# Edge logits through a DRAM table instead of one-hot matmuls in a graph network kernel

## The chip, the cores and the metric

The kernel runs on one core of a Trainium2 chip. The metric is device time in microseconds (us) for one execution. The engines of the core are PE (TensorE, matrix products; PEld is its weight load), DVE (VectorE), ACT (ScalarE), POOL (GpSimd) and SP (SyncE, here only a queue of transfers). DMA transfers run beside them.

## The reference, cut to what matters

512 nodes with 1024 features and 8192 edges, sorted by destination. The edges are of three kinds by their position: the first 256 are `hh`, the next 1280 `oo`, the last 6656 `ho`. Only the attention part concerns the change:

```python
h = relu(layernorm(x))
feat  = concat([h[src], h[dst]])                 # per edge, 2048 wide
e     = relu(feat @ W_kind + b_kind)             # one weight per kind of edge
logit = (e @ W_a + b_a)[:, 0]
m     = segment_max(logit, dst);  ex = exp(logit - m[dst])
alpha = ex / segment_sum(ex, dst)[dst]
z     = segment_sum(alpha[:, None] * h[src], dst)
out1  = x + relu(concat([h, z]) @ W_node + b_node)   # W_hn for the first 128 rows, W_on for the others
# then a second graph layer on out1: layernorm, relu, one linear map, sums with degree weights
```

Two edges of one kind with the same source and destination have the same logit. So the kernel keeps, for each kind, a dense 512 x 512 matrix of logits (destination by source) and one of edge counts, and does the softmax and the sum over edges as dense matrix work.

## The kernel before, in words

**Tables.** `feat @ W_kind` is split into a source half and a destination half. For each of the three kinds and each half, PE multiplies all 512 nodes, so an edge needs only one row of `tab_a` (source) and one of `tab_b` (destination, bias added), both in DRAM. That is 12 *edge chunks* of PE work (numbers 0 to 11: kind, half, half of the columns), then four *node chunks* (12 to 15) for the upper halves of `W_on` and `W_hn`. A chunk has 8 *steps* (k = 0 to 7); a step is one 256 KB weight load on SP's queue into one of 8 slots of `raw` (L247), a rounding to a high part on ACT (L448), the low part on DVE (`low_w`, L897), and 12 matmuls on PE (L646; fewer in a node chunk). ACT or DVE copies each finished bank to `stage` (L466, L905) and ACT's queue stores it, 1 MB per edge chunk. A load is released by the low part 8 steps before it, so the loads follow DVE's order.

**Counts.** In chunks 2 to 5 DVE makes two 0/1 matrices per tile of 128 edges (`count_onehots`), and PE sums their products into the counts.

**Gathers.** There are 64 tiles of 128 edges: 52 `ho`, 10 `oo`, 2 `hh`, in that order. For tile q POOL issues an indirect DMA that fetches 128 rows of `tab_a` (4 KB each) into one of 8 slots of `gath` (`gather_src`, L308) and, when that has landed, a second one that fetches 128 rows of `tab_b` and adds them in SBUF (`gather_dst`, L315), three tiles later in the order. Before each `gather_src` POOL copies the tile's indices to `tabl_s` (L305). DVE's `edge(q)` (L912) then does relu, the product with `W_a` and the row sum, which gives 128 logits in `lg[:, q]`, and frees the slot.

**Sums.** The logits go to the dense matrix by matmul. DVE splits them into three bf16 parts (`split_logits`, L918 to L923) and makes two one-hot matrices (`logit_onehots`, L929); ACT scales one by each part (`logit_parts`, L495); PE adds three products per tile, 12 per step being the weights' own (`add_logits`, L596). DVE also prepares the inverse of the counts (L935, L936) and a mask for pairs without an edge (L941), which PE adds (`open_masked`, L615), and at the end of each kind multiplies and takes row maxima (`copy_kind`, L947). Tables of numbers (`SUM_AT`, `EDGE_AT`, `ONEHOT_AT`, `SPLIT_AT`) say at which chunk and step each of these stands: seven tiles per chunk in chunks 6 to 11, the rest in chunks 12 to 15, and `edge(q)` 12 steps ahead of its sum.

**After that.** DVE combines the row maxima (L1021 to L1023; `nmx` is the last), ACT takes exponentials, DVE the row sums, and from there the kernel is one chain: attention product, node update, second layer, output. Nothing of it is touched by the change.

Of the kernel before, what the change touches and what calls it, by code (L numbers as in the profile page):

```python
# [5 lines left out]
P = 128  # L25
# [19 lines left out]
def gnn_kernel(nc, x, src, dst, W_hh, b_hh, W_oo, b_oo, W_ho, b_ho, W_a, b_a,  # L45
# [12 lines left out]
    with ExitStack() as ctx:  # L58
# [8 lines left out]
        def sb(name, shape, dt, size=None, over=None, shift=0):  # L67
# [6 lines left out]
            else:  # L74
# [16 lines left out]
        G, TC = 8, 7  # L91
        topsum = sb("topsum", [P, NM, D], F32)
        onehot = sb("onehot", [P, OS, 4, N], BF16, over="topsum")
# [13 lines left out]
        GROUPS = {g: -(-ET // g) for g in (G, TC)}  # L107
        pow8 = sb("pow8", [1, G, G + 3], F32)
        code_row = sb("code_row", [1, ET + G], F32)
        code_w = sb("code_w", [1, ET + G], F32)  # L110
        pack_f = sb("pack_f", [1, G + 3], F32)

        pack_i = {g: sb(f"pack{g}_i", [1, GROUPS[g]], I32) for g in (G, TC)}
        node_f = sb("node_f", [P, ET, 3], F32)
        tabl_f = sb("tabl_f", [P, ET, 2], F32, over="logit_d", shift=20 * P)
        tabl_i = sb("tabl_i", [P, ET, 2], U32)
        tabl_s = sb("tabl_s", [P, GB, 2], U32)
        lg = sb("lg", [P, ET], F32)
        lgr = sb("lgr", [P, ET], F32)
        lgp = sb("lgp", [P, 3, ET], BF16)  # L120
        lgs = sb("lgs", [P, 3, ET], F32)
# [26 lines left out]
        mask_b = [sb("mask_ho", [P, NM, N], BF16, over="logit_d", shift=4 * (2 * NM * N + 2 * N)),  # L148
                  sb("mask_oo", [P, NM, N], BF16, over="bias2", shift=4 * D),
                  sb("mask_hh", [P, NM, N], BF16, over="bias2")]  # L150
# [7 lines left out]
        top_d = nc.dram_tensor("top_d", [N, D], F32).ap()  # L158

# [13 lines left out]
        s_mask = sem("masks_ready")  # L173
        s_part = sem("onehot_parts_ready")
# [18 lines left out]
        s_stg = sem("index_staged")  # L193
        s_seen = sem("index_seen")
        s_oh = sem("onehots_ready")
        s_ohu = sem("onehot_slots_free")
        s_kind = sem("kind_counted")
        s_kfree = sem("kind_banks_free")
# [27 lines left out]
        TILES = (T_HO, T_OO, T_HH)  # L226
        CH_EDGE = 3 * 2 * NN
# [45 lines left out]
        def _(pool):  # L273
# [10 lines left out]
                           allow_small_or_imprecise_dtypes=True).then_inc(s_gconst, 1)  # L284
            for j in range(G):
                nc.gpsimd.memset(pow8[:, j, :], float(8 ** j)).then_inc(s_gconst, 1)
            nc.gpsimd.memset(code_row[:, :], 0.0).then_inc(s_gconst, 1)
            nc.gpsimd.memset(ones[:, :], 1.0).then_inc(s_gconst, 1)
            for m in range(NM):
                pool.wait_ge(s_x[m], 16)  # L290
            pool.dma_start(wa_b[:, :], W_a.rearrange("d a -> a d").partition_broadcast(P)).then_inc(s_const, 16)
# [10 lines left out]
            def gather_src(q, s, kinds):  # L302

                pool.wait_ge(s_edge, q + 1)
                nc.gpsimd.tensor_copy(tabl_s[:, s, :], tabl_i[:, bass.ds(q, 1), :].rearrange("p a b -> p (a b)")).then_inc(s_stg, 1)  # L305
                pool.wait_ge(s_stg, q + 1)
                pool.sem_inc(s_seen, 1)
                pool.indirect_dma_start(out=gath[:, s, :], out_offset=None, in_=tab_a[0:kinds * N, :],  # L308
                                        in_offset=bass.IndirectOffsetOnAxis(ap=tabl_s[:, s, 0:1], axis=0)).then_inc(s_ga[s], 16)

            def gather_dst(s, u, kinds):

                pool.wait_ge(s_ga[s], u * 16 + 16)
                pool.sem_inc(s_seen, 1)
                pool.indirect_dma_start(out=gath[:, s, :], out_offset=None, in_=tab_b[0:kinds * N, :],  # L315
                                        in_offset=bass.IndirectOffsetOnAxis(ap=tabl_s[:, s, 1:2], axis=0),
                                        compute_op=ALU.add).then_inc(s_g[s], 16)
# [5 lines left out]
            def gather_run(first, end, kinds, pending=0):  # L323

                for q in range(first, end):
                    gather_src(q, q % GB, kinds)
                    if q - LAG >= first - pending:
                        gather_dst((q - LAG) % GB, (q - LAG) // GB, kinds)

            def gather_rest(end, kinds):  # L330
                for q in range(end - LAG, end):
                    gather_dst(q % GB, q // GB, kinds)

            LAG = 3
            for i in range(4):
                pool.wait_ge(s_st[i], 32)
            for q in range(GB):
                gather_src(q, q, 1)
            tables_landed(1)
            pool.wait_ge(s_copied, NM + NM * 4)  # L340
            for q in range(GB - LAG):
                gather_dst(q, 0, 1)
            bias(0, b_hh)
            with pool.Fori(1, T_HO // GB) as i:
                for s in range(GB):
                    gather_src(i * GB + s, s, 1)
                    gather_dst((s - LAG) % GB, i if s >= LAG else i - 1, 1)
            gather_run(T_HO // GB * GB, T_HO, 1, LAG)
            gather_rest(T_HO, 1)
            tables_landed(2)  # L350
            gather_run(T_HO, T_HO + T_OO, 2)
            gather_rest(T_HO + T_OO, 2)
            tables_landed(3)
# [5 lines left out]
            pool.wait_ge(s_ohu, OS + 2 * ET)  # L359
# [29 lines left out]
        SUM_AT = {(6 + i, k): i * TC + k for i in range(6) for k in range(TC)}  # L389
        SUM_AT |= {(12, k): 42 + k for k in range(8)}  # L390
        SUM_AT |= {(13, k): 50 + k for k in range(2)}
        SUM_AT |= {(13, 4 + k): 52 + k for k in range(4)}
        SUM_AT |= {(14, k): 56 + k for k in range(6)}
        SUM_AT |= {(15, k): 62 + k for k in range(2)}
        assert sorted(SUM_AT.values()) == list(range(ET))

        EARLIER = 12
        EDGE_AT = {divmod(c * KT + k - EARLIER, KT): q for (c, k), q in SUM_AT.items() if q < ET - 2} | {(14, 0): ET - 2, (14, 1): ET - 1}
        ONEHOT_AT = {divmod(c * KT + k - 1, KT): q for (c, k), q in SUM_AT.items() if q < ET - 2} | {(14, 6): ET - 2, (14, 7): ET - 1}

        SPLIT_AT = {}
        for c in range(6, 16):
            tiles = [q for (c2, _), q in SUM_AT.items() if c2 == c]
            SPLIT_AT[(c - 1, KT - 1) if c < 15 else (14, 4)] = (min(tiles), max(tiles) + 1)

        SLOT, SLOT_FREE, user = {}, {}, {s: ET - OS + s for s in range(OS)}
        for (_, k), q in sorted(SUM_AT.items()):
            SLOT[q] = k % OS
            SLOT_FREE[q] = OS + user[k % OS] + 1
            user[k % OS] = ET + q  # L410
        LAST_OF_KIND = (T_HO - 1, T_HO + T_OO - 1, ET - 1)
# [7 lines left out]
        def _(act):  # L419
# [40 lines left out]
            def copy_a(q):  # L460

                for m in range(NM):
                    bank_done(act, q, m)
                    if q:
                        act.wait_ge(s_st[m], q * 16)
                    nc.scalar.copy(stage[:, m, :], ps[:, NM + m, :]).then_inc(s_copied, 1)  # L466
                    act.wait_ge(s_copied, NM + q * NM + m + 1)
                    act.dma_start(table(q, m), stage[:, m, :]).then_inc(s_st[m], 16)
# [21 lines left out]
            def logit_parts(q):  # L490

                act.wait_ge(s_oh, ET + q + 1)
                s = SLOT[q]
                for i in (1, 2, 0):
                    ins = nc.scalar.mul(onehot[:, s, 1 + i, :], onehot[:, s, 1, :], lgs[:, i, q:q + 1])  # L495
                ins.then_inc(s_part, 1)

# [7 lines left out]
            def edge_chunk(q):  # L505

                for k in range(KT):
                    if q * KT + k + AHEAD < (CH_EDGE + 4) * KT:
                        rounds(q * KT + k + AHEAD, q * KT + k + AHEAD + 1)
                    if (q, k) in SUM_AT:  # L510
                        logit_parts(SUM_AT[q, k])
# [65 lines left out]
        def _(pe):  # L577
            pe.sem_inc(s_slot, KT)
            pe.sem_inc(s_ohu, OS)
            pe.wait_ge(s_gconst, 7 + G)  # L580

            def codes(g, size):

                return nc.values_load_multi_w_load_instructions(
                    pack_i[size][0:1, bass.ds(g, 1)], engines=[mybir.EngineType.PE], min_val=0, max_val=8 ** size - 1,
                    skip_runtime_bounds_check_because="the codes are packed on the chip, 3 bits each")[1][0]

            def accumulate(code, t, s, parts):
# [5 lines left out]
                def block(j):  # L594
                    for i in range(parts):
                        mm = nc.tensor.matmul(ps[:, bass.ds((lo + j) & 3, 1), :].rearrange("p a n -> p (a n)"),  # L596
                                              onehot[:, s, 1 + i, j * P:(j + 1) * P], onehot[:, s, 0, :],
                                              start=False, stop=False, skip_group_check=True)
                    return mm
# [10 lines left out]

            def open_masked(t):

                pe.wait_ge(s_mask, t + 1)
                for b in range(NM):
# [565 lines left out]
```

## Time and profile before

| | us |
|---|---|
| median of 3 runs | 665.55 |
| the 3 runs | 665.55, 665.29, 667.62 |
| span of the profiled execution | 665.7 |

| engine | busy us | share of the span | instructions |
|---|---|---|---|
| PE | 571.4 | 86% | 2440 |
| DVE | 442.1 | 66% | 903 |
| ACT | 287.4 | 43% | 466 |
| POOL | 217.7 | 33% | 228 |

The profile gives no time of the profiled execution other than its span from the first to the last instruction; it agrees with the median of the runs. Busy times are sums over stages with different limits, so each stage has to be read by itself. A DMA share is the busy share of the 16 DMA engines; it can read a little over 1 because packets of different queues overlap.

### The profile page before, as it was taken

How to read it: one execution, taken by the hardware profiler on the slowest of the kernel's cores; microseconds unless marked ns; L12 is line 12 of the kernel's file. 1: busy time of each engine (PE TensorE's matmuls, PEld its weight loads, DVE VectorE, ACT ScalarE, POOL GpSimd, SP SyncE). 2: the span in 40 equal slices, each digit the busy share in tenths (PEclk: the TensorE clock that was granted, in tenths of full speed). 3: DMA queues.
4: the chain of work that ended last, by engine and by line, in shares of the span. 5: the costliest groups of instructions: out<-in, count | busy, mean ns of one | idle time of the engine just before them, and what ended most of it. 6: DMA issues, size and time to landing. Idle time of an engine off the chain costs nothing.

```text
span 665.7 us, 8504 instructions
## 1 busy us (share of the span) xinstructions
PE 571.4 (86%) x2440; PEld 424.7 (64%) x2441; DVE 442.1 (66%) x903; ACT 287.4 (43%) x466; POOL 217.7 (33%) x228
## 2 busy tenths in 40 slices
PE   0899999999949995969697998667949999879987
PEld 0788777776626674647475666434738788768876
DVE  6715266775776987867878975686795289872152
ACT  2623312113175554547473555589853182142110
POOL 2000230186775766667653676310030000000000
PEclk9899999999969997988989899788978899989989
DMA  8335483499999999999999999983455076030021
GB/s 316 129 111 175 135 307 122 150 224 323 301 298 314 291 314 299 310 305 317 298 318 281 323 295 308 257 226 111 128 198 213 16 247 228 2 126 0 1 79 48
DMA packets 54727, 140.53 MB, mean 211 GB/s; under 512 B 6050, under 2 KB 6178, under 8 KB 54690
## 3 DMA queue, kind: packets, MB, share of 16 engines
q0 software_dynamic: 20624, 74.98, 41.7%
q1 hardware_dynamic: 25824, 50.34, 21.8%
q10 hardware_dynamic: 8242, 14.75, 5.9%
q8 instruction: 19, 0.31, 0.2%
q14 instruction: 18, 0.15, 0.1%
HBM read 123.27 MB, written 16.78 MB: 210 GB/s over the span
## 4 chain that ended last, share of the span: by engine, by line
PE 42%; DMA 23%; POOL 12%; issue 10%; DVE 8%; ACT 3%; POOLq 1%; DVEq 0%
PE ps L646 23%; DMA gath<-tab_a,tabl_s 19%; POOL gath L315 7%; PE ps L632 6%; POOL gath L308 3%; PE ps L826 3%; DMA gath<-tab_b,tabl_s 3%; PE ps L596 3%; PE ps L782 2%; POOL tabl_s L305 2%; ACT onehot L495 2%; PE ps L803 2%; DVE logit_d L947 1%; DVE logit_d L1036 1%; PE ps L625 1%
## 5 line engine op out<-in xcount | busy, mean ns | idle before, releaser
L646 PE MATMUL ps<-ring_h,actT_h 128*128 128x512 f32 x520 | 228.3, 439 | 34.4 <-ACT stage L466 15.8
L646 PE MATMUL ps<-ring_h,actT_l 128*128 128x512 f32 x520 | 209.0, 402 | 0.0
L646 PE MATMUL ps<-ring_l,actT_h 128*128 128x512 f32 x520 | 208.4, 401 | 0.0
L495 ACT ACTIVATE onehot<-onehot,lgs 128x512 bf16<-128x512 bf16 x192 | 124.6, 711 | 104.2 <-DVE onehot L929 104.2
L646 PEld LDWEIGHTS ps<-ring_h,actT_h 128*128 128x128 f32 x520 | 101.6, 195 | 68.1 <-ACT stage L466 17.7
L315 POOL DMA_INDIRECT gath<-tab_b,tabl_s x64 | 105.7, 1652 | 95.8 <-DMA gath<-tab_a,tabl_s 40.4
L448 ACT CAST ring_h<-raw 128x512 fp32r<-128x512 f32 x160 | 94.8, 614 | 87.8 <-PE ps L646 70.7
L912 DVE SCALAR_TENSOR_TENSOR gath<-gath,wa_b 128x1024 f32<-128x1024 f32 x64 | 78.0, 1219 | 67.6 <-DMA gath<-tab_b,tabl_s 67.6
L897 DVE TENSOR_TENSOR ring_l<-raw,ring_h 128x512 fp32r<-128x512 f32 x160 | 106.6, 685 | 16.5 <-ACT ring_h L448 16.4
L646 PEld LDWEIGHTS ps<-ring_h,actT_l 128*128 128x128 f32 x520 | 101.0, 194 | 22.9
L646 PEld LDWEIGHTS ps<-ring_l,actT_h 128*128 128x128 f32 x520 | 101.8, 196 | 20.9
L596 PE MATMUL ps<-onehot 128*128 128x512 bf16 x292 | 83.8, 396 | 18.1 <-ACT onehot L495 15.7
L308 POOL DMA_INDIRECT gath<-tab_a,tabl_s x64 | 78.9, 1232 | 50.7 <-POOL tabl_s L305 47.3
L305 POOL COPY tabl_s<-tabl_i 128x2 uint32 (+1 forms) x64 | 50.1, 783 | 70.1 <-DMA tab_a<-stage 64.5
L596 PEld LDWEIGHTS ps<-onehot 128*128 128x128 bf16 x292 | 21.8, 100 | 61.3 <-issue 49.7
L848 DVE TENSOR_SCALAR onehot<-iota_f,node_f 128x512 bf16<-128x512 f16 x64 | 23.6, 369 | 31.3 <-PE ps L596 31.3
L936 DVE RECIPROCAL logit_d<-logit_d 128x512 f32<-128x512 f32 x12 | 40.2, 3353 | 0.4
L929 DVE TENSOR_SCALAR onehot<-iota_f,node_f 128x512 bf16<-128x512 f16 x128 | 39.3, 350 | 1.6 <-PE ps L596 1.2
L890 DVE TENSOR_TENSOR actT_l<-ps,actT_h 128x512 fp32r<-128x512 f32 x24 | 16.4, 691 | 31.7 <-ACT actT_h L440 31.7
L440 ACT CAST actT_h<-ps 128x512 fp32r<-128x512 f32 x24 | 14.0, 588 | 42.6 <-PE ps L632 34.7
L466 ACT COPY stage<-ps 128x512 f32<-128x512 f32 x24 | 14.0, 585 | 25.8 <-PE ps L646 19.1
L560 ACT CAST ring_h<-ps 128x512 fp32r<-128x512 f32 x16 | 8.8, 591 | 34.4 <-PE ps L782 12.7
(160 smaller groups left out, 517.3 us busy)
## 6 DMA issues: line engine op xcount, KB each, us to landing
raw<-in_L_gnn_W_ho_dram SPq DMA_DIRECT2D x32, 256.0 KB, 3.9
raw<-in_L_gnn_W_oo_dram SPq DMA_DIRECT2D x32, 256.0 KB, 6.8
raw<-in_L_gnn_W_hh_dram SPq DMA_DIRECT2D x32, 256.0 KB, 7.3
raw<-in_L_gnn_W_on_dram SPq DMA_DIRECT2D x32, 256.0 KB, 4.8
raw<-in_L_gnn_W_hn_dram SPq DMA_DIRECT2D x32, 256.0 KB, 4.0
tab_a<-stage ACTq DMA_DIRECT2D x24, 256.0 KB, 7.4
tab_b<-stage ACTq DMA_DIRECT2D x24, 256.0 KB, 8.1
w1row<-in_L_gnn_W_dram SPq DMA_DIRECT2D x2, 2048.0 KB, 8.9
```

The costliest lines, as they stand in the source:

```text
L305: nc.gpsimd.tensor_copy(tabl_s[:, s, :], tabl_i[:, bass.ds(q, 1), :].rearrange("p a b -> p (a b)")).then_inc(s_stg, 1)
L308: pool.indirect_dma_start(out=gath[:, s, :], out_offset=None, in_=tab_a[0:kinds * N, :], in_offset=bass.IndirectOffsetOnAxis(ap=tabl_s[:, ...
L315: pool.indirect_dma_start(out=gath[:, s, :], out_offset=None, in_=tab_b[0:kinds * N, :], in_offset=bass.IndirectOffsetOnAxis(ap=tabl_s[:, ...
L448: nc.scalar.copy(ring_h[:, k, :], raw[:, k % RAW, :]).then_inc(s_high, 1)
L495: ins = nc.scalar.mul(onehot[:, s, 1 + i, :], onehot[:, s, 1, :], lgs[:, i, q:q + 1])
L596: mm = nc.tensor.matmul(ps[:, bass.ds((lo + j) & 3, 1), :].rearrange("p a n -> p (a n)"), onehot[:, s, 1 + i, j * P:(j + 1) * P], onehot[: ...
L632: mm = nc.tensor.matmul(ps[:, b, :], w, v, start=(i == 0), stop=(i == len(pairs) - 1))
L646: mm = nc.tensor.matmul(ps[:, first + m, :], w, v, start=(k == 0 and i == 0), stop=(k == KT - 1 and i == 2))
L897: nc.vector.tensor_tensor(ring_l[:, k, :], raw[:, k % RAW, :], f32(ring_h[:, k, :]), ALU.subtract).then_inc(s_low, 1)
L912: nc.vector.scalar_tensor_tensor(out=gath[:, s, :], in0=gath[:, s, :], scalar=0.0, in1=wa_b[:, :], op0=ALU.max, op1=ALU.mult, accum_out=lg ...
L929: ins = nc.vector.tensor_scalar(onehot[:, SLOT[q], j, :], iota_f[:, :], node_f[:, q, e:e + 1], None, ALU.is_equal)
L936: nc.vector.reciprocal(logit_d[:, t, k, :], logit_d[:, t, k, :])
```

## The change

The sums by matmul are gone, and with them everything that prepared them: the three bf16 parts, the one-hots per logit tile, ACT's scaling, the inverse counts, the masks, the copies per kind, and the tables that placed them. The counts are still made as before.

Instead there is a table `pair_d` in DRAM with one float for each kind, destination and source (3 x 512 x 512, 3 MB). POOL fills `stage` with -1e30 at the start and stores it three times over the table. A third column of the index table holds kind x 512 x 512 + dst x 512 + src. When `edge(q)` has run, POOL scatters `lg[:, q]`, 128 floats of 4 bytes, into the table by an indirect DMA. A scatter waits until the scatter before it has landed. When all tiles of a kind are scattered, POOL reads that kind's 1 MB back into `logit_d`, and DVE takes row maxima over it with three reductions; `b_a` is added once in the maxima.

POOL's loop is written out and no longer copies indices: in each round it issues the scatter of tile q - 8, the source gather of tile q and the destination gather of tile q - 3. `edge(q)` stands at step 38 + 3q/2 of DVE's list (step 8c + k is chunk c, step k), the last four after the last chunk. ACT's first copy to `stage` waits for the fill.

```diff
-            for q in range(T_HO + T_OO, ET):
-                gather_src(q, q % GB, 3)
-            for q in range(T_HO + T_OO, ET):
-                gather_dst(q % GB, q // GB, 3)
...
+            def scatter(q):
+
+                pool.wait_ge(s_edge, GB + q + 1)
+                t = kind_of(q)
+                if q > FIRST_OF[t]:
+                    pool.wait_ge(s_sc[t], 16 * (q - FIRST_OF[t]))
+                elif t:
+                    pool.wait_ge(s_sc[t - 1], 16 * TILES[t - 1])
+                pool.indirect_dma_start(out=pair_d, out_offset=bass.IndirectOffsetOnAxis(ap=tabl_i[:, q, 2:3], axis=0),
+                                        in_=lg[:, q:q + 1], in_offset=None).then_inc(s_sc[t], 16)
+
+            def logits_back(t):
+
+                pool.wait_ge(s_sc[t], 16 * TILES[t])
+                pool.dma_start(logit_d[:, t, :, :], pairs[t].rearrange("(m p) s -> p m s", p=P)).then_inc(s_lg[t], 16)
...
+            pool.wait_ge(s_fill, 48)
+            for q in range(GB, ET + LAG):
+                if q == T_HO:
+                    tables_landed(2)
+                if q == T_HO + T_OO:
+                    tables_landed(3)
+                if q - BACK >= 0:
+                    scatter(q - BACK)
+                if q < ET:
+                    gather_src(q, 1 + kind_of(q))
+                gather_dst(q - LAG, 1 + kind_of(q - LAG))
+                if q == T_HO + T_OO - 1:
+                    logits_back(0)
+            for q in range(ET + LAG - BACK, ET):
+                scatter(q)
+            logits_back(1)
+            logits_back(2)
...
-        SUM_AT = {(6 + i, k): i * TC + k for i in range(6) for k in range(TC)}
...
+        EDGE_STEPS = [38 + q * 3 // 2 for q in range(ET)]
...
             with pe.Fori(0, 6) as i:
-                edge_chunk(i + 6, before=lambda k: uniform_sums(i, k))
+                edge_chunk(i + 6)
...
-                    if (q, k) in INVERSE_AT:
-                        inverse_counts(*INVERSE_AT[q, k])
-                    if (q, k) in MASK_AT:
-                        make_mask(MASK_AT[q, k])
-                    if (q, k) in ((13, 2), (15, 2)):
-                        copy_kind(q - 13)
-                    if (q, k) in EDGE_AT:
-                        edge(EDGE_AT[q, k])
-                    if (q, k) in SPLIT_AT:
-                        split_logits(*SPLIT_AT[q, k])
-                    if (q, k) in ONEHOT_AT:
-                        logit_onehots(ONEHOT_AT[q, k])
-                    if (q, k) == (14, 7):
-                        copy_kind(1)
-
-
-            dve.wait_ge(s_kfree, 3 * NM)
+                    for e in EDGES_AT.get((q, k), ()):
+                        edge(e)
+            for e in range(ET):
+                if EDGE_STEPS[e] >= (CH_EDGE + 4) * KT:
+                    edge(e)
+
+
+            for t in range(3):
+                dve.wait_ge(s_lg[t], 16)
+                ins = nc.vector.tensor_reduce(mx3[:, t, :], logit_d[:, t, :, :], AX.X, ALU.max)
+            step(ins)
             step(nc.vector.tensor_tensor(mx[:, :], mx3[:, 0, :], mx3[:, 1, :], ALU.max))
```

POOL's order in the middle of the gathers, before; each round is an index copy, a source gather and a destination gather:

```order
L305 COPY tabl_s<-tabl_i 128x2
L308 DMA gath<-tab_a,tabl_s 128x1024
L315 DMA gath<-tab_b,tabl_s 128x1024
L305 COPY tabl_s<-tabl_i 128x2
L308 DMA gath<-tab_a,tabl_s 128x1024
L315 DMA gath<-tab_b,tabl_s 128x1024
```

The same place after the change (its line numbers are those of the changed kernel); `pair_d<-lg` is the scatter:

```order
L305 DMA pair_d<-lg,tabl_i 786432x1
L287 DMA gath<-tab_a,tabl_i 128x1024
L293 DMA gath<-tab_b,tabl_i 128x1024
L305 DMA pair_d<-lg,tabl_i 786432x1
L287 DMA gath<-tab_a,tabl_i 128x1024
L293 DMA gath<-tab_b,tabl_i 128x1024
```

In every round the scatter stands where the copy stood, ahead of both gathers, and it waits for the landing of the scatter one round earlier.

The end of POOL's gathers after the change; the last row with x5 is scatters 59 to 63, and the x2 are the reads of the second and third kind:

```order
L305 DMA pair_d<-lg,tabl_i 786432x1
L287 DMA gath<-tab_a,tabl_i 128x1024
L293 DMA gath<-tab_b,tabl_i 128x1024
L305 DMA pair_d<-lg,tabl_i 786432x1
L293 DMA gath<-tab_b,tabl_i 128x1024
L305 DMA pair_d<-lg,tabl_i 786432x1
L293 DMA gath<-tab_b,tabl_i 128x1024
L305 DMA pair_d<-lg,tabl_i 786432x1
L293 DMA gath<-tab_b,tabl_i 128x1024
L305 DMA pair_d<-lg,tabl_i 786432x1 x5
L311 DMA logit_d<-pair_d 128x4x512 x2
```

The last destination gather is followed by five scatters in a row and two reads, where before the gathers ended POOL's part.

DVE's order ahead of `nmx` after the change (`gath,lg<-gath,wa_b` is `edge`, `ring_l<-raw,ring_h` is the low part of a weight step):

```order
L819 TENSOR_TENSOR ring_l<-raw,ring_h 128x512
L834 SCALAR_TENSOR_TENSOR gath,lg<-gath,wa_b 128x1024
L819 TENSOR_TENSOR ring_l<-raw,ring_h 128x512 x2
L834 SCALAR_TENSOR_TENSOR gath,lg<-gath,wa_b 128x1024
L819 TENSOR_TENSOR ring_l<-raw,ring_h 128x512
L834 SCALAR_TENSOR_TENSOR gath,lg<-gath,wa_b 128x1024 x5
L897 TENSOR_REDUCE mx_86<-logit_d 128x4 x3
L899 TENSOR_TENSOR mx<-mx_86 128x4
L900 TENSOR_TENSOR mx<-mx,mx_86 128x4
L901 TENSOR_SCALAR mx<-mx,ba 128x4
L902 TENSOR_SCALAR nmx<-mx,ba 128x4
```

The last low part of chunk 15 stands behind edge 58, and edges 59 to 63 and the three reductions follow it; before, edges 62 and 63 stood in chunk 14.

## Rows read from the trace of the kernel before

**Rows 1.** The page's 40 slices of the span: busy tenths, and GB/s moved.
```profile
PE   0899999999949995969697998667949999879987
DMA  8335483499999999999999999983455076030021
GB/s 316 129 111 175 135 307 122 150 224 323 301 298 314 291 314 299 310 305 317 298 318 281 323 295 308 257 226 111 128 198 213 16 247 228 2 126 0 1 79 48
```

**Rows 2.** Busy time by stage: stage, length, each engine, granted PE clock, DMA share, GB/s.
```profile
core 0: us, PE busy (x) PEld busy (x) DVE busy (x) ACT busy (x) POOL busy (x), PEclk, DMA share, GB/s
0.00:26.00 26.00, 6.44 (x32) 6.25 (x33) 16.20 (x33) 11.42 (x17) 4.78 (x24) 1.00 0.60 224
...
137.00:426.00 289.00, 247.62 (x1021) 173.38 (x1020) 218.89 (x432) 144.38 (x233) 184.84 (x171) 0.92 1.05 301
426.00:477.00 51.00, 40.42 (x152) 23.61 (x151) 36.93 (x100) 45.11 (x74) 5.05 (x3) 0.90 0.60 177
477.00:666.00 189.00, 166.01 (x758) 136.38 (x756) 113.33 (x190) 57.82 (x95) 5.91 (x11) 0.93 0.29 105
```

**Rows 3.** Vector engine in time order: first edge, last edge, `nmx` (start, duration).
```profile
136.92 1.23 DVE L912 SCALAR_TENSOR_TENSOR gath<-gath,wa_b 128x1024 f32<-128x1024 f32 x1 [0.17 <-DMA gath<-tab_b,tabl_s]
...
446.94 1.22 DVE L912 SCALAR_TENSOR_TENSOR gath<-gath,wa_b 128x1024 f32<-128x1024 f32 x1
...
476.52 0.17 DVE L1023 TENSOR_SCALAR nmx<-mx 128x4 f32<-128x4 f32 x1
```

**Rows 4.** DMA queues from 137 to 426 us (packets, MB, engine share), then two issues.
```profile
q0 software_dynamic: 16683, 60.75, 80.1%
q1 hardware_dynamic: 9659, 17.59, 17.2%
q10 hardware_dynamic: 4608, 8.39, 7.7%
...
raw<-in_L_gnn_W_hh_dram SPq DMA_DIRECT2D x32, 256.0 KB, 7.3
...
gath<-tab_b,tabl_s POOLq DMA_INDIRECT x59, 15.7
```

**Rows 5.** DMA queues from 426 to 477 us.
```profile
q1 hardware_dynamic: 3013, 5.50, 32.9%
q0 software_dynamic: 587, 2.13, 19.3%
q10 hardware_dynamic: 720, 1.31, 7.0%
```

**Rows 6.** Groups by line, whole span: count, busy us, mean ns, idle before, releaser.
```profile
L495 ACT ACTIVATE onehot<-onehot,lgs 128x512 bf16<-128x512 bf16 x192 | 124.6, 711 | 104.2 <-DVE onehot L929 104.2
...
L912 DVE SCALAR_TENSOR_TENSOR gath<-gath,wa_b 128x1024 f32<-128x1024 f32 x64 | 78.0, 1219 | 67.6 <-DMA gath<-tab_b,tabl_s 67.6
...
L596 PE MATMUL ps<-onehot 128*128 128x512 bf16 x292 | 83.8, 396 | 18.1 <-ACT onehot L495 15.7 <-issue 2.4
...
L936 DVE RECIPROCAL logit_d<-logit_d 128x512 f32<-128x512 f32 x12 | 40.2, 3353 | 0.4
L929 DVE TENSOR_SCALAR onehot<-iota_f,node_f 128x512 bf16<-128x512 f16 x128 | 39.3, 350 | 1.6 <-PE ps L596 1.2
...
L1052 DVE TENSOR_TENSOR adj<-adj,count_d 128x2048 f32<-128x2048 f32 x1 | 2.3, 2293 | 0.0
```

**Rows 7.** One round of POOL in time order (start, duration, idle before).
```profile
159.16 0.97 POOL L308 DMA_INDIRECT gath<-tab_a,tabl_s  x1 [0.79 <-POOL tabl_s L305]
160.44 1.55 POOL L315 DMA_INDIRECT gath<-tab_b,tabl_s  x1 [0.31 <-issue]
```

**Rows 8.** The page's DMA issues: count, KB each, median us from issue to landing.
```profile
gath<-in_x_dram SPq DMA_DIRECT2D x4, 512.0 KB, 5.2
top_d<-stage ACTq DMA_DIRECT2D x8, 256.0 KB, 2.6
```

More of the change, by code:

```diff
@@ L172, in gnn_kernel @@
         s_topl = [sem(f"top_loaded{m}") for m in range(NM)]
-        s_mask = sem("masks_ready")
-        s_part = sem("onehot_parts_ready")
+        s_neg = sem("empty_pairs_made")
+        s_fill = sem("pairs_filled")
+        s_sc = [sem(f"logits_scattered{t}") for t in range(3)]
+        s_lg = [sem(f"logits_loaded{t}") for t in range(3)]
         s_pool = sem("pool_chain")
@@ L321, in tables_landed @@
                     pool.wait_ge(s_st[i], 64 * kinds)
[L323 to L332, printed above, removed]
             LAG = 3
+            BACK = GB
             for i in range(4):
@@ L337, in _ @@
             for q in range(GB):
-                gather_src(q, q, 1)
+                gather_src(q, 1)
             tables_landed(1)
@@ L386, in gnn_kernel @@
         LAST_COUNTS = FIRST_COUNTS + ET // (2 * KT) - 1
-        SUM_AT = {(6 + i, k): i * TC + k for i in range(6) for k in range(TC)}
[L390 to L411, printed above, removed]
+        EDGE_STEPS = [38 + q * 3 // 2 for q in range(ET)]
+        EDGES_AT = {}
+        for q, at_step in enumerate(EDGE_STEPS):
+            EDGES_AT.setdefault(divmod(at_step, KT), []).append(q)
         def is_a(q):
@@ L579, in _, with codes, accumulate @@
             pe.sem_inc(s_ohu, OS)
-            pe.wait_ge(s_gconst, 7 + G)
-            def codes(g, size):
+            pe.wait_ge(s_gconst, 6 + G)
+            def codes(g):
                 return nc.values_load_multi_w_load_instructions(
-                    pack_i[size][0:1, bass.ds(g, 1)], engines=[mybir.EngineType.PE], min_val=0, max_val=8 ** size - 1,
+                    pack_i[0:1, bass.ds(g, 1)], engines=[mybir.EngineType.PE], min_val=0, max_val=8 ** G - 1,
                     skip_runtime_bounds_check_because="the codes are packed on the chip, 3 bits each")[1][0]
-            def accumulate(code, t, s, parts):
+            def accumulate(code, t, s):
                 lo = code >> (3 * t)
                 def block(j):
[L595 to L599, printed above, removed]
+                    return nc.tensor.matmul(ps[:, bass.ds((lo + j) & 3, 1), :].rearrange("p a n -> p (a n)"),
+                                            onehot[:, s, 1, j * P:(j + 1) * P], onehot[:, s, 0, :],
+                                            start=False, stop=False, skip_group_check=True)
                 with pe.If((lo & 4) > 0):
@@ L609, in open_banks @@
                     nc.tensor.matmul(ps[:, b, :], zeros_r[:, 0:P], zeros_r[:, :], start=True, stop=False, skip_group_check=True)
-            def open_masked(t):
-                pe.wait_ge(s_mask, t + 1)
-                for b in range(NM):
-                    nc.tensor.matmul(ps[:, b, :], ident_b[:, :], mask_b[t][:, b, :], start=True, stop=False, skip_group_check=True)
             def close_banks(done):
@@ L735, in _ @@
                     free = lambda m: pe.wait_ge(s_copied, waits[c] + (m if c == 0 else 0))
-                chunk(q + c, NM, ms, free, before=lambda k: last_sums(q + c, k))
-            pe.wait_ge(s_kfree, 3 * NM)
+                chunk(q + c, NM, ms, free)
+            pe.wait_ge(s_ccopy, 3)
             q += 4
```

165 lines of the change are left out of this document (46 added, 119 removed).

## The prediction, on record before the changed kernel ran

> **What bounds the kernel now.** I read the 40 slices first, then the busy times by stage, then the DMA queues of two stages, and last DVE's list around `nmx`. The page's totals point at PE, at 86%. The slices say otherwise for the part that the change touches: from slice 9 to slice 26 the DMA row is all nines while PE drops to 4 to 7 in several of them [rows 1]. By stage, the 289 us from the first `edge` at 137 us to 426 us have a DMA share of 1.05 at 301 GB/s, PE busy for 248 us, DVE for 219, ACT for 144 [rows 2, 3]. Only the transfers have no room there. The very first slice, plain loads, moved 316 GB/s [rows 1], so 301 is near what these engines give. DVE's `edge` waits 67.6 us for the second gather [rows 6], and that gather takes 15.7 us from issue to landing [rows 4]: a deep queue. So the middle of the kernel is bound by DMA, and POOL's queue q0 alone, the gathers, is 80.1 of the 105 points [rows 4].
>
> After 426 us this turns. From 426 to 477 us the DMA share is 0.60, and ACT is busy for 45 of 51 us [rows 2]: there the chain is one-hots, scaling, products, up to `nmx`, which ends at 476.7 us [rows 3]. From 477 us on, 189 us are the chain that the change leaves alone [rows 2]. So the new time is the old one plus the shift of `nmx`.
>
> **What the change removes, and why little of it counts.** ACT loses 192 scalings, 124.6 us. PE loses three of every four of the 292 one-hot products (three parts against one for the counts), 83.8 x 3/4 = 63 us. DVE loses 128 one-hots, 39.3 us, and 12 reciprocals, 40.2 us [rows 6], and smaller things. Until 426 us all this stands beside saturated transfers and returns nothing. What it can return at most is the stretch after the gathers, 51 us, if the transfers of that stretch cost nothing. But they do not vanish.
>
> **DMA work up to the last gather.** DVE's list keeps edges and weight steps in one order, and the last edges now stand at the end of chunk 15, so nearly all loads and stores that the kernel before moved by 477 us must now be moved before the last gather. In engine time: 1.05 x 289 = 303.5 us, and 0.60 x 51 = 30.6 us [rows 2], of which loads are 32.9% of 51, 16.8 us [rows 5]. Sum 334.1.
>
> Added: the read of the first kind, 1 MB. A 256 KB store takes 7.7% of 289 us over 8.39 MB, 0.70 us each [rows 4], so 1 MB is 2.8 us. Then 64 scatters of 128 packets of 4 bytes, 8 packets per engine. No row shows such a packet. From below it is nothing, 512 bytes in all. From above it is as dear as a packet of q10, which are of 2 KB nearly all: 7.7% of 289 us x 16 engines / 4608 = 77 ns, 8 x 77 = 0.62 us per scatter. Packet time follows bytes in the rows (q0, mostly 4 KB and half of them adding, 222 ns by the same division), so I take a value near the lower end, 0.15 us: 64 x 0.15 = 9.6 us (0 to 40). Together 334.1 + 2.8 + 9.6 = 346.5 us.
>
> I divide by 1.03 rather than by 1.05, because q0 will no longer hold a deep queue (next part) and an engine that runs out early idles: 336 us (330 at 1.05, 346 at 1.00). From 137 us that is 473. Plus 1 us at the start: `edge(0)` moves from step 36 to 38, while five destination gathers are queued (0 to 5, with the 3 MB fill, 12 x 0.70 = 8.3 us in the first 26 us, where the share is 0.60 [rows 2] and where loads and the first rows could be late). Plus 3 us for the last three rounds, which have no source gather to fill the queue (1 to 6). The last gather lands at 477 us.
>
> **The tail behind it.** Scatter 59 lands right behind the last gather, 0.3 us. Scatters 60 to 63 wait for one another. One takes an issue on POOL like a source gather, 1.0, the 0.3 us of idle that POOL shows before an instruction that waits for nothing [rows 7], and a landing; a store of 256 KB takes 2.6 us [rows 8], less its 0.70 of transfer, 1.9; plus 0.1. That is 3.3 us, four times, 13.2. Behind POOL's last scatter wait both reads. The second kind's is hidden; the third's takes 0.9 of issue, 2.8 of transfer, 1.9 of landing, 5.6 us (the 512 KB loads took 5.2 [rows 8]). DVE's third reduction over 2048 elements takes about what the sum over 2048 does, 2.3 [rows 6]; four small operations 0.8, by the 0.17 of `nmx` and the steps between [rows 3]. Tail 22.2 us (16 to 30). So `nmx` ends at 477 + 22 = 499.5 us instead of 476.7: 23 us later.
>
> The profiled execution has a span of 665.7 us, the median of the runs is 665.55, so I carry the difference over unchanged: **688 us**. The index copies that POOL loses (0.79 us of idle behind each [rows 7]) are off the path: a round of scatter, source and destination gather is 1.3 + 1.3 + 1.9 = 4.5 us of POOL, below the 336 / 63 = 5.3 us of DMA work per tile.
>
> **Does the chain of scatters set the pace?** It is the one new wait in the loop. When scatter n lands, both gathers issued behind it are still in q0 (taking q0 as served in order), 5.3 us of engine time less the landing, 1.9. The next source gather is queued 0.3 + 1.0 + 0.3 + 1.0 = 2.6 us later. 1.9 + 2.6 = 4.5, under 5.3, so the engines do not run dry, with 0.8 us to spare. If landings were as slow as loads in this stage (7.3 us against 2.6 for the unloaded store [rows 4, 8]), they would.
>
> The Trainium skill ("DMA: Bandwidth & Descriptors", section "Latency and other measured facts") puts HBM access at 0.2 us on average and 2 us under high load, and says that this is most of a DMA's fixed cost. By that rule the landing here would be up to 1.8 us longer; no row shows a small write under load, so it speaks for the first rival below and changes no term.
>
> **Rivals.**
> A, the scatter chain sets the pace. For it: loaded landings are long. Against: part of the gap is filled by loads and stores (25 of 105 points [rows 4]). It decides from a landing of 2.7 us on. At 3.5 us, 0.8 us per round over 58 rounds, 46 us at most and about 35 after the filling: 723 us.
> B, scatter packets are as dear as 2 KB packets: (0.62 - 0.15) x 64 / 1.03 = 29 us more, 717 us. The Trainium skill (same page, "Specifications") says that below 512 B a DMA engine does a read-modify-write, which speaks for B; no trace here shows what that costs.
> C, everything small: scatters at 0.05, share 1.05, tail 17. (336.9 + 3.2) / 1.05 = 324, 137 + 324 + 1 + 17 = 479 us, 2 us later: 668 us, no change to tell.
> D, faster: the engine time of the gathers is itself stretched by the work that is removed (ACT's and DVE's traffic, and the 3.4 us reciprocals that hold back the freeing of slots [rows 6]). Place: 137 to 426 us. The best slices there move 323 GB/s against 301 [rows 1, 2], and I allow 10%: 346.5 / 1.155 = 300, 137 + 300 + 4 + 22 = 463 us, 14 us earlier: 652 us. It decides from about 6% on. Against: the share stays at its height through all 18 slices, whatever DVE and ACT do.
>
> **How the numbers follow.** The forecast's mechanism (DMA work plus tail) has 0.57, with a range of its own from 672 to 706; A 0.16, B 0.10, C 0.07, D 0.10. A difference under 0.5%, 3.3 us, cannot be told from none. Faster comes from D: 0.10. Same comes from C: 0.07. Slower is the rest, 0.83. The range from 666 to 728 leaves out D and the far end of A and B.
>
> **What would show it.** Right: DMA nines from slice 9 to about slice 28 with nothing below; PE and ACT much less busy at the same span or more; `edge` waiting longer for the second gather; last gather near 477 us; then five scatters about 3.3 us apart with PE, ACT and DVE idle; `nmx` near 500; 189 us behind it as before. A shows in q0 running dry in each round, with DMA at 7 or 8 and POOL waiting for scatters; B in a q0 share that grows with unchanged bytes; D in more GB/s in the gather stage. Wrong altogether: gathers that end before 455 us, or a tail behind `nmx` that is not 189 us.

## The result, and the profile after

The changed kernel takes **734.0 us** (median of 6 runs, 728.0 to 737.6) against 665.5 for the kernel before on the same chip: a ratio of 1.098, 95% interval 1.093 to 1.103. It is slower, as forecast, but by 68 us and not by 23, and outside the range of 666 to 728. The profiled execution has a span of 726.0 us.

The stages of the kernel after, in the columns of [rows 2] (stretch and length, busy time of PE, PEld, DVE, ACT and POOL with counts, granted PE clock, DMA share, GB/s): up to the last gather, the tail up to the end of `nmx`, and the rest:

```profile
137.00:515.00 378.00, 254.50 (x956) 191.88 (x954) 153.96 (x276) 68.05 (x109) 221.40 (x178) 0.82 0.98 257
515.00:537.80 22.80, 0.00 (x0) 0.00 (x0) 8.49 (x10) 5.17 (x5) 5.65 (x6) 0.50 0.28 92
537.80:726.00 188.20, 158.21 (x720) 129.78 (x720) 113.78 (x191) 57.87 (x95) 5.78 (x11) 0.90 0.29 102
```

The tail and the last stretch are as forecast: 23.1 us from the last gather to `nmx` (22.2 forecast), and 188.2 behind it (189). The whole miss stands in the first row. The last gather lands at 514.7 us, not at 477. ACT and DVE are far less busy than in the same stage of before [rows 2], which brings nothing. The DMA share is 0.98, hardly below the 1.05 of before, but the rate fell from 301 to 257 GB/s. The page's slices show both at once, as in [rows 1]; PEclk is the granted clock:

```profile
PE   0899999999888698774957434463004999969987
PEclk9999999999999799986979555766555999989999
DMA  8734843899999999999999999998336416430011
GB/s 342 290 113 142 299 151 120 202 326 231 281 288 255 274 259 268 275 247 231 281 253 285 262 247 239 233 266 198 51 116 242 151 58 216 161 116 0 1 59 58
```

Nines in the DMA row from slice 9 to slice 27, as before, but from slice 10 on over 231 to 288 GB/s, where the kernel before mostly moved 281 to 323. Whoever reads the digits alone sees a saturated queue. The reason is in POOL's list. Two rounds of its loop (start, duration, and the idle time before it with what ended it; L305 is the scatter, L287 the source gather, L293 the destination gather):

```profile
441.31 1.06 POOL L305 DMA_INDIRECT pair_d<-lg,tabl_i  x1 [0.55 <-DVE gath L834]
442.68 0.98 POOL L287 DMA_INDIRECT gath<-tab_a,tabl_i  x1 [0.30 <-issue]
443.96 1.57 POOL L293 DMA_INDIRECT gath<-tab_b,tabl_i  x1 [0.30 <-issue]
448.09 1.51 POOL L305 DMA_INDIRECT pair_d<-lg,tabl_i  x1 [2.56 <-DMA pair_d<-lg,tabl_i]
449.91 0.97 POOL L287 DMA_INDIRECT gath<-tab_a,tabl_i  x1 [0.30 <-issue]
```

POOL issues three transfers in 4.2 us and then stands before the next scatter until the last one has landed; both gathers behind it wait with it. From the first scatter at 143.0 us to the 60th at 511.87 there are 59 rounds, 6.25 us each on average; where a scatter waits only for the one four before it, they take 5.16 on average (first experiment). All 64 scatters together, with what POOL waited for:

```profile
  DVE gath L834: 62.9, 32
  DMA pair_d<-lg,tabl_i: 62.1, 29
  issue: 3.0, 3
```

Half of it is put down to `edge` on DVE. That is a reading to distrust: the instruction waits on two semaphores, the edge named is a later tile's, and for the scatter at 441.31 us the edge that it needs had ended some 17 us earlier. The trace's packets (the pieces of at most 4 KB in which a DMA engine moves a transfer) say what ended the wait: in 58 of the 59 rounds POOL starts a scatter 1.2 to 2.1 us after the last packet of the scatter before it, and in the quiet tail, where nothing else can hold it, 1.1 to 1.3 us after. In the first experiment only the landing's wait is moved back, the one for the edge stays, and the DVE share of the idle time falls from 62.9 to 13.8 us.

The tail behind the last gather (POOL, then DVE; L311 reads the table, L897 reduces, L902 is `nmx`) has the length that the prediction gave it, with scatters 2.9 to 3.1 us apart once nothing else is in the queue:

```profile
515.63 1.16 POOL L305 DMA_INDIRECT pair_d<-lg,tabl_i  x1 [2.68 <-DMA pair_d<-lg,tabl_i]
518.71 0.96 POOL L305 DMA_INDIRECT pair_d<-lg,tabl_i  x1 [1.92 <-DMA pair_d<-lg,tabl_i]
521.57 0.96 POOL L305 DMA_INDIRECT pair_d<-lg,tabl_i  x1 [1.90 <-DMA pair_d<-lg,tabl_i]
524.45 0.96 POOL L305 DMA_INDIRECT pair_d<-lg,tabl_i  x1 [1.92 <-DMA pair_d<-lg,tabl_i]
```

```profile
514.71 1.23 DVE L834 SCALAR_TENSOR_TENSOR gath<-gath,wa_b 128x1024 f32<-128x1024 f32 x1 [2.63 <-DMA gath<-tab_b,tabl_i]
...
534.61 2.29 DVE L897 TENSOR_REDUCE mx<-logit_d 128x4 f32<-128x2048 f32 x1 [0.34 <-DMA logit_d<-pair_d]
...
537.59 0.23 DVE L902 TENSOR_SCALAR nmx<-mx,ba 128x4 f32<-128x4 f32 x1
```

### The profile page after: what moved, and what is told of

It reads as the page before. It is cut to its first block, busy times and chain, and to the rows that moved or that the text cites. A ratio compares the mean times of both kernels' runs of the same rounds, so it can differ in the third digit from the quotient of the medians.

```text
span 726.0 us, 7020 instructions
## 1 busy us (share of the span) xinstructions
PE 529.6 (73%) x2197; PEld 412.4 (57%) x2198; DVE 349.6 (48%) x661; ACT 171.3 (24%) x274; POOL 256.8 (35%) x234
## 2 busy tenths in 40 slices
DMA packets 58014, 146.75 MB, mean 202 GB/s; under 512 B 8194, under 2 KB 8322, under 8 KB 57602
## 4 chain that ended last, share of the span: by engine, by line
DMA 39%; PE 37%; DVE 9%; issue 7%; POOL 7%; ACT 1%; POOLq 0%; DVEq 0%
DMA gath<-tab_b,tabl_i 23%; PE ps L598 21%; DMA pair_d<-lg,tabl_i 15%; PE ps L584 5%; POOL pair_d L305 3%; DVE gath L834 3%; POOL gath L287 3%; PE ps L748 3%; PE ps L704 2%; PE ps L725 2%; PE ps L555 2%; DMA logit_d<-pair_d 1%; DVE logit_d L915 1%; DVE stats L789 1%; DVE hrow_l L908 1%
## 5 line engine op out<-in xcount | busy, mean ns | idle before, releaser
L598 PE MATMUL ps<-ring_h,actT_h 128*128 128x512 f32 x520 | 224.7, 432 | 108.0 <-DVE ring_l L819 68.7
L598 PE MATMUL ps<-ring_l,actT_h 128*128 128x512 f32 x520 | 213.8, 411 | 0.0
L598 PE MATMUL ps<-ring_h,actT_l 128*128 128x512 f32 x520 | 213.5, 411 | 0.0
L293 POOL DMA_INDIRECT gath<-tab_b,tabl_i x64 | 102.7, 1605 | 62.4 <-DMA tab_b<-stage 43.2
L305 POOL DMA_INDIRECT pair_d<-lg,tabl_i x64 | 72.6, 1134 | 127.9 <-DVE gath L834 62.9
L287 POOL DMA_INDIRECT gath<-tab_a,tabl_i x64 | 64.3, 1005 | 80.4 <-DMA tab_a<-stage 61.2
L664 PE MATMUL ps<-ident,logit_d 128*128 128x128 f32 x16 | 4.4, 433 | 55.4 <-ACT logit_d L499 55.4
L770 DVE TENSOR_SCALAR onehot<-iota_f,node_f 128x512 bf16<-128x512 f16 x64 | 23.1, 360 | 41.8 <-PE ps L555 37.4
L408 ACT CAST actT_h<-ps 128x512 fp32r<-128x512 f32 x24 | 13.8, 589 | 42.9 <-PE ps L584 34.1
L771 DVE TENSOR_SCALAR onehot<-iota_f,node_f 128x512 bf16<-128x512 f16 x64 | 22.7, 354 | 0.0
L555 PE MATMUL ps<-onehot 128*128 128x512 bf16 x73 | 21.6, 384 | 0.5 <-issue 0.3
L577 PE MATMUL ps<-ident,hrow 128*128 128x128 f32 x32 | 5.7, 362 | 17.5 <-ACT hrow L403 17.5
```

Source lines behind the costliest of these rows:

```text
L287: pool.indirect_dma_start(out=gath[:, q % GB, :], out_offset=None, in_=tab_a[0:kinds * N, :], in_offset=bass.IndirectOffsetOnAxis(ap=tabl_ ...
L293: pool.indirect_dma_start(out=gath[:, q % GB, :], out_offset=None, in_=tab_b[0:kinds * N, :], in_offset=bass.IndirectOffsetOnAxis(ap=tabl_ ...
L305: pool.indirect_dma_start(out=pair_d, out_offset=bass.IndirectOffsetOnAxis(ap=tabl_i[:, q, 2:3], axis=0), in_=lg[:, q:q + 1], in_offset=No ...
L555: return nc.tensor.matmul(ps[:, bass.ds((lo + j) & 3, 1), :].rearrange("p a n -> p (a n)"), onehot[:, s, 1, j * P:(j + 1) * P], onehot[:, ...
L598: mm = nc.tensor.matmul(ps[:, first + m, :], w, v, start=(k == 0 and i == 0), stop=(k == KT - 1 and i == 2))
L770: nc.vector.tensor_scalar(onehot[:, s, 0, :], iota_f[:, :], node_f[:, q, 0:1], None, ALU.is_equal)
```

## The experiments

Theory 1: the wait for the last scatter's landing, once in each round, starves the gather queue. Theory 2: the scatters' small writes load the DMA engines. Theory 3: DVE's steps or PE's clock pace the stage. Each ratio is to the kernel before on the same chip.

**Four tables in rotation (e1).** A scatter waits only for the one four before it. Only the first table is filled and read back, so three quarters of the logits are left out.

```
-                if q > FIRST_OF[t]:
-                    pool.wait_ge(s_sc[t], 16 * (q - FIRST_OF[t]))
+                if q >= 4:
+                    pool.wait_ge(s_sc[q % 4], 16 * (q // 4))
-                pool.indirect_dma_start(out=pair_d, ...
+                pool.indirect_dma_start(out=pair_t[q % 4], ...
```

> The scatters go in turn to four tables, so a scatter waits for the one four tiles earlier instead of the one before it; all 64 scatters and their packets stay. Only the first table is filled and read back, so the logits of the other three quarters of the tiles are left out of the result. Theory 1 (in each round of the loop POOL waits for the last scatter to land, and q0 runs short of work): the rounds fall from 6.1 us to about 5.3, the last gather lands near 477 us instead of 514, the five last scatters no longer wait for one another (about 10 us less behind the last gather), time about 688 us (680 to 700). Theory 2 (the small writes to DRAM slow the engines down for the gathers behind them): the rounds stay at 6.1 us, only the end gains, about 724 us. Theory 3 (the scatter has no part in it; the edge steps or the lower PE clock pace the rounds): also about 724 us.

Measured: 663.4 us, ratio 0.994 (0.992 to 0.997). Last gather at 456.8 us; the 59 rounds from the first scatter to the 60th take 5.16 us on average. One of the shortest, 4.5 us with no wait (L304 is the scatter here), and the stage up to the last gather in the columns of the first fence:

```profile
304.51 1.01 POOL L304 DMA_INDIRECT pair_d<-lg,tabl_i  x1 [0.30 <-issue]
305.83 0.98 POOL L289 DMA_INDIRECT gath<-tab_a,tabl_i  x1 [0.30 <-issue]
307.11 1.56 POOL L295 DMA_INDIRECT gath<-tab_b,tabl_i  x1 [0.30 <-issue]
308.97 1.01 POOL L304 DMA_INDIRECT pair_d<-lg,tabl_i  x1 [0.30 <-issue]
```

```profile
137.00:458.00 321.00, 242.79 (x963) 184.36 (x961) 155.40 (x278) 68.83 (x109) 231.69 (x182) 0.87 1.05 304
```

The same 64 scatters and gathers, 57.9 us sooner. Theories 2 and 3 are out as the main cause; theory 1 gave the direction, and the time came out 17 us below its range.

**No scatters at all (e2).** The logits are not placed; fill and read stay.

```
-                if q - BACK >= 0:
-                    scatter(q - BACK)
```

> All 64 scatters and their waits are left out; the table is still filled and read back, so the logits are left out of the result. Theory 1: like the run with four tables, rounds of about 5.3 us, last gather near 475 us, about 680 us (670 to 692). Theory 2: the same, about 680 us. Theory 3: rounds stay at 6.1 us and only the end behind the last gather gains some 13 us, about 720 us.

Measured: 657.2 us, ratio 0.986 (0.983 to 0.990), where theories 1 and 2 had both said about 680; last gather at 453.8 us, only 3.0 us before e1's. Its stage:

```profile
137.00:455.00 318.00, 241.61 (x955) 183.71 (x953) 153.88 (x277) 68.32 (x108) 154.31 (x119) 0.88 1.05 308
```

1.05 x 318 = 334 us of engine time, against 1.05 x 321 = 337 with scatters. So 64 scatters that nothing waits for cost some 3 us, 0.05 each; the shares are rounded to 0.01, which is 3 us here, so this is an estimate, but the last gather too is only 3.0 us later. Theory 2's scatters are nearly free.

**The wait alone put back (e5).** Four tables as in e1, but each scatter waits for the last one, in another table. Left out is what e1 leaves out.

```
-                if q >= 4:
-                    pool.wait_ge(s_sc[q % 4], 16 * (q // 4))
+                if q:
+                    pool.wait_ge(s_sc[(q - 1) % 4], 16 * ((q - 1) // 4 + 1))
```

> The kernel with four DRAM tables in rotation (663.4 us), with one thing put back: each scatter again waits until the last one, into another table, has landed. Only the first table is filled and read back, so the output is another. Theory 1 (the wait by itself makes the loss): the time of the changed kernel, 734 us (725 to 742), rounds of 6.1 us, last gather at about 515 us. Rival (four tables helped because the writes were spread over more DRAM, or because two scatters no longer met in one table): near 663 us, under 680.

Measured: 736.1 us, ratio 1.105 (1.099 to 1.111), the changed kernel's time. What POOL waited for at its 64 scatters, and the stage up to the last gather at 522.3 us:

```profile
  DMA pair_d<-lg,tabl_i: 77.0, 31
  DVE gath L834: 56.4, 27
```

```profile
137.00:523.00 386.00, 259.40 (x964) 194.81 (x962) 154.99 (x277) 68.71 (x109) 219.99 (x179) 0.81 0.97 253
```

This differs from e1 in one wait, and that wait is the loss. Spreading the writes over four tables has no share in it.

**Two tables, the whole computation (v3).** Even tiles in one table, odd in the other, both filled and read, DVE takes the maximum (the fill is -BIG).

```
+                dve.wait_ge(s_lg[t], 32)
+                nc.vector.tensor_tensor(logit_d[:, t, :, :], logit_d[:, t, :, :], two, ALU.max)
```

> The changed kernel with two DRAM tables, even tiles scattered into one and odd tiles into the other, each scatter waiting for the one two before it in its own table; both tables are filled, both are read back and VectorE takes the larger of the two, so the whole computation is done. Theory 1 (a wait for the last scatter's landing in each round starves the gather queue): the scatter two rounds back landed long ago, so rounds are 5.0 us as with four tables, last gather at about 457 to 462 us; two more reads and three maxima of some 2.3 us in the tail and 3 MB more to fill early: 672 us (664 to 682). Rival (a landing takes more than two rounds, or four tables helped by spreading the writes): rounds of 5.5 us or more, 695 us or above.

Measured: 676.9 us, ratio 1.015 (1.011 to 1.019). Last gather at 460.4 us, as theory 1 said, with rounds of 5.3 us on average where it had 5.0; the tail to `nmx` is 25 us with its two more reads and the maxima. So the chain's loss is gone, and what is left is a kernel that still does not beat the one before: `nmx` ends at 485.9 us, 9 us later than in the kernel before [rows 3], because the transfers that stood behind the gathers there now stand ahead of the last gather, and the tail follows. One reading was not expected, POOL's waits at the scatters:

```profile
  DMA pair_d<-lg,tabl_i: 38.0, 22
```

Even the scatter two rounds back has often not landed. A landing is no fixed time: with more gathers queued ahead of it, it takes longer. From the end of POOL's issue to a scatter's last packet it is 3.7 us in the changed kernel, 7.5 here and 12.8 in e1 (means of the first 60 scatters, counted in the traces' packets), and 0.8 in the quiet tail of the changed kernel. Here the wait harms little, the last gather being 3.6 us later than in e1, since two rounds of gathers are queued behind it.

**Plain gathers, one table (v1).** The destination gather goes plainly into its own slot and DVE adds the two; six pairs of slots. The chain stays.

```
-                                        compute_op=ALU.add).then_inc(s_g[q % GB], 16)
+                                        ).then_inc(s_g[q % GP], 16)
+                step(nc.vector.tensor_tensor(slot_a(q), slot_a(q), slot_b(q), ALU.add))
```

> The changed kernel with plain gathers: the second gather goes to a slot of its own and DVE adds the two rows (one more pass of 1.2 us per tile); six pairs of slots in place of eight slots; both gathers of a tile are issued in the same round; the chain of scatters stays. The adding packets take about twice as long as plain ones (327 against 159 ns in the trace of before), so 64 x 8 x 0.168 = 86 us of engine time go. Theory 1: the rounds are then set by POOL (3.9 us) and by the landing of the scatter, about 4.5 us, last gather near 425 us, about 645 us (620 to 670). Theory 2: engine time of about 4.1 us per tile plus what the scatters cost, about 0.8, the same 645 us. Theory 3 (edge steps): 1.5 steps of 2.75 us, 4.1 us per tile, about 620 us.

Measured: 692.0 us, ratio 1.036 (1.031 to 1.042), a miss by 47 us: I had taken less DMA work for less time, while the chain set the pace. POOL's scatters waited 85.5 us for landings, and the share in the stage was 0.87 at 290 GB/s.

**Plain gathers and two tables (v2).** Both edits, the whole computation; the scatter's part:

```
+                if q >= NT:
+                    pool.wait_ge(s_sc[q % NT], 16 * (q // NT))
+                pool.indirect_dma_start(out=pair_t[q % NT], ...      # NT = 2
```

> The same two tables, and the destination gather is a plain one into a slot of its own, VectorE adding the two (six pairs of slots). Theory 1: the chain held the plain gathers at 692 us with the queue at 57 to 62% of the engines; without it the queue runs until the engines or the table stage bound it, rounds of 4.1 to 4.6 us, last gather at 400 to 435 us, 640 us (615 to 660). Rival (the plain gathers are held by VectorE's extra add or by six pairs of slots, not by the chain): rounds stay at 5 us or above, 675 us or more.

Measured: **643.8 us, ratio 0.964 (0.959 to 0.969)**, better than both kernels. The stage to the last gather at 428.4 us:

```profile
137.00:429.00 292.00, 241.57 (x962) 183.38 (x960) 230.45 (x340) 68.30 (x109) 201.32 (x180) 0.89 0.93 339
```

The rate is 339 GB/s, and POOL now waits for free slots, 34.9 us, and 5.0 us for landings.

**Plain gathers in the kernel before (b1).** The eight slots of before make four pairs; the space of v2's last pairs is filled there by masks and inverse counts.

```
-                pool.indirect_dma_start(out=gath[:, s, :], out_offset=None, in_=tab_b...
+                pool.indirect_dma_start(out=gath[:, 4 + s % 4, :], out_offset=None, in_=tab_b...
```

> The kernel before (logits placed by one-hot matmuls, no scatter) with plain destination gathers: four pairs of slots in the same eight, VectorE adds the two. It asks whether the gain of the version with two tables and plain gathers (643.8 us) needs the change at all. If the adding gathers alone bound the kernel before: 64 packets' worth of time less, 640 us (620 to 655). Rival (four pairs are too shallow a ring, POOL waits for VectorE's steps in each round): 665 us or more.

Measured: 672.5 us, ratio 1.011 (1.007 to 1.014). The stage:

```profile
137.00:440.00 303.00, 256.70 (x1041) 177.96 (x1039) 297.32 (x515) 153.34 (x247) 161.64 (x181) 0.91 0.87 302
```

DVE is busy for 297 of 303 us: the adds meet the one-hots, reciprocals and masks that the change removes. So the freed DVE time has a use after all, but only with plain gathers. How much of b1 is DVE and how much the shallow ring was not separated.

**A plain 512-byte store in the scatter's place, same waits (e3).** The logits go in order into a DRAM tensor that nobody reads.

```
-                pool.indirect_dma_start(out=pair_d, out_offset=..., in_=lg[:, q:q + 1], ...)
+                pool.dma_start(lg_d[q * P:(q + 1) * P, :], lg[:, q:q + 1]).then_inc(s_sc[t], 16)
```

> Each scatter is replaced by a plain store of the same 512 bytes to one contiguous place in DRAM, with the same waits in the same order; the logits are left out of the result. Theory 1 (the wait in each round): as the changed kernel, about 734 us (722 to 740). Theory 2 (128 single writes all over the table): rounds fall toward 5.3 us, about 695 us. Theory 3: about 734 us.

Measured: 1001.7 us, ratio 1.495 (1.488 to 1.501), where theory 1 had said 734. The store, meant as a twin of the scatter, is another thing (L306 is the store):

```profile
308.68 0.60 POOL L306 DMA_DIRECT2D lg_d<-lg  x1 [5.58 <-DMA lg_d<-lg]
...
321.80 0.60 POOL L306 DMA_DIRECT2D lg_d<-lg  x1 [9.33 <-DMA lg_d<-lg]
```

**The same store, waiting for the one four before (e4).**

```
+                if q >= 4:
+                    pool.wait_ge(s_sc[q % 4], 16 * (q // 4))
                 pool.dma_start(lg_d[q * P:(q + 1) * P, :], lg[:, q:q + 1]).then_inc(s_sc[q % 4], 16)
```

> The kernel with plain 512-byte stores of a tile's logits in place of the scatters (1001.7 us with the wait for the last one in each round), now with a wait only for the store four before; the logits are not placed in the table, so the output is another. Theory 1 (the store's long landing, 7 to 8 us and more, waited for in each round, made the 1001.7 us): 665 us (655 to 685), rounds of 5 us. Rival (the stores themselves hold the DMA engines or the queue): 850 to 1000 us.

Measured: four runs from 771 to 817 us, between both theories and too far apart for a ratio. By the shortest alone, the wait makes some 230 us of e3's loss (1001.7 - 771.3), and the stores the rest: (771 - 663) / 64 = 1.7 us for each store, by e1's 663.4 us. This is an estimate. It does not stand in the stores' own packets, of which the page counts as many as for scatters (8194 under 512 bytes in the changed kernel, e3 and e4 alike), but in those of the gathers: up to the last gather, q0's packets took 73.6% of 628 us in e3, 462 us, for 64.0 MB, and in the changed kernel 273 us for 63.8 MB. Why 128 adjacent 4-byte writes cost so much more than 128 scattered ones stays open; address and queue were not varied.

## Why the prediction was wrong

**The step that failed is "Does the chain of scatters set the pace?"** It took the landing as 1.9 us, from a store in a quiet stage [rows 8], and concluded that the engines do not run dry, "with 0.8 us to spare"; it put the turning point at 2.7 us. Measured: 6.25 us per round, less 1.1 of issue and 0.3 of POOL's usual gap, is 4.8 us from the issue's end until POOL goes on. In the quiet tail the same reckoning gives 1.9 - 0.3 = 1.6. That the wait makes the loss is shown by e5, which differs from e1 in it alone. The mistake has a form: the step pictured the gathers queued behind the scatter and forgot those queued ahead of it. The packets show them: a scatter's last packet runs 3.7 us after its issue in this stage, and later the more is queued ahead (v3, e1).

The Trainium skill ("DMA: Bandwidth & Descriptors", section "Anatomy of one DMA — SWDGE (gpsimd) path") gives some 2.0 us of fixed cost for such a transfer, setup and completion together. The trace agrees for the last scatter of all, 2.1 us from issue to landing. By the Trainium skill (same page, section "Latency and other measured facts"), where HBM access takes 0.2 us on average and 2 us under high load, load would add up to 1.8 us, an estimate. An estimate by both, 3.8 us, is 2.1 short of the 1.1 + 4.8 = 5.9 us of this stage.

Rival A was therefore right, with 0.16. Its price, 723, was short: it reckoned 0.8 us per round, 46 us, and took off a quarter for other loads that fill the gap. The runs show 514.7 - 456.8 = 57.9 us, and 8 us more in the tail (23.1 against e1's 15.4, whose last scatters do not wait for one another). That the price came near is luck, for its rule does not hold either: with 4.8 us in place of 3.5, a turning point of 2.7 gives 2.1 us per round, 122 us over 58 rounds. The rule lets the gathers behind a scatter run while it waits for its landing. Here a scatter's first packet runs 2.1 us after its issue and its last 3.7 (the same means), and up to then the engines work on what was queued ahead of it.

Of the signs that I named for A, POOL waited for scatters, but a DMA share of 7 or 8 did not show. Up to the last gather the changed kernel moved 97.2 MB and e1 97.5, and the engines were busy for 0.98 x 378 = 370 us against 337. The queues of both say where, the changed kernel first (packets, MB, share of 16 engines):

```profile
q0 software_dynamic: 19414, 63.77, 72.1%
q1 hardware_dynamic: 12960, 23.60, 19.0%
```

```profile
q0 software_dynamic: 19564, 63.99, 75.8%
q1 hardware_dynamic: 13024, 23.71, 20.9%
```

q0 took 0.721 x 378 = 273 us for what took 0.758 x 321 = 243: with few gathers queued, the mean packet lasts 12% longer. Not every packet does. Most 4 KB packets of q0 take 159 or 327 ns in both kernels; but in the changed one 1195 of 15558 take more than 345 ns, in e1 21 of 15612, and what those 1195 have above e1's mean of 246 ns adds up to the 30 us. So the loss splits into 33 / 1.05 = 31 us of such packets and 370 / 0.98 - 370 / 1.05 = 25 of a lower share, and the busy digits hide it, since they count a long packet as work. The queue does run thin: from 160 to 500 us fewer than 8 packets of q0 were under way for 24% of the time, in e1 (160 to 440) for 8%. What the long packets wait for was not tested.

**The other steps.**
- DMA work as the bound of the gathers: right. The 334.1 us carried over from before and 2.8 for the read, 336.9, are 334 in e2. But 301 GB/s was not "near what these engines give": with plain gathers v2 moved 339 up to its last gather.
- Scatters at 0.15 us, 9.6 in all: mis-sized, some 3 us (0.05 each). Rival B is out. The page counts 58014 packets in the changed kernel and 55966 without scatters, 32 for each scatter and not the 128 that were priced.
- Division by 1.03: wrong without the chain (1.05 in e1 and e2) and with it (0.98). Together with the scatters' term and the 4 us for the start and the last rounds, this put the last gather 20 us too late for a kernel without a chain (457 against 477). Chain and sum thus err in opposite ways: -20 + 58 + 1 in the tail - 1 behind it is the 38 us between 688 and the span of 726.
- What ACT, PE and DVE lose returns nothing in this kernel: right, e1 and v3 bear it out. Rival D is out: with the chain gone the rate is 304 GB/s, 301 before.
- The 189 us behind `nmx`: right. The tail, 23.1 us against 22.2, came out by luck: 11.8 us from the last gather to the last scatter's landing instead of 13.5, and 8.1 from there to the third reduction instead of 5.6 (the 0.9 of issue in it stood in no row; it took 0.8). The second kind's read is not hidden: POOL issues it behind the last scatter, at 525.41 us, 1.4 us ahead of the third's.

## What to carry to other kernels

In these runs a small transfer landed behind what its queue held already. So a wait for its landing, on the engine that also issues the large transfers, must be priced from a loaded landing, and it keeps the queue short; give the chain a second and third buffer before the loop depends on it. Read saturation from GB/s beside the busy digits: in the starved queue of this kernel a few packets took much longer and kept the digits at nine. Work taken off an engine that does not bound pays once the bound is moved: the scatter's freed DVE time and slots became a gain only with plain gathers and no chain.

## What the runs showed of the hardware that was not expected

- An indirect scatter of 128 elements of 4 bytes costs the engines some 0.05 us; a plain store of the same 512 bytes into adjacent DRAM words costs this kernel about 1.7 us (an estimate from e4's shortest run), and in e3 POOL waited 6.6 us for its landing on average, with nothing else to do.
- A gather that adds in SBUF is dear: v2's q0 moved 57.9 MB between 137 and 400 us at a share of 59.7%, e1's q0 58.0 MB between 137 and 430 at 75.0%. That is 157 us against 220 for the same bytes. In the packets, too: with one gather of two adding, the 4 KB packets of the kernel before take some 159 or some 327 ns, about half each; in v2, where none adds, 50 of 15961 take 320 to 345 ns and most 159.
